# A graph, attention and expert layer on one core: degree factor at the projection's PSUM, and a rewritten end of the edge stage

## The reference

```python
xn = layernorm(x)
# 1. edges
m    = xn[src] @ W[:256] + edge_attr @ W[256:]
deg  = segment_sum(ones, dst)
norm = where(deg > 0, rsqrt(maximum(deg, 1)), 0)
h    = segment_sum(m * norm[dst][:, None], dst) + h_bias
# 2. linear attention, 8 heads of 32, and an MLP
q, k, v = split((xn @ w_qkv + b_qkv) per head);  k, v = ln(k), ln(v)
ret = q @ (k.T @ v / 6250) + xn
mix = gelu(ret @ w1 + b1) @ w2 + b2 + xn
x   = x + h + mix
# 3. two of eight experts, chosen once for all nodes
z      = layernorm(x)
logits = mean(z over nodes) @ Wr + br           # 8 numbers
...                                             # softmax, capacity factor, softmax, top 2, softmax
out    = w_a * expert_a(z) + w_b * expert_b(z)  # 256 -> 512 -> gelu -> 256, each with biases
x      = x + layernorm(out + z) * gamma + beta
```

## Time and profile before

| | |
|---|---|
| runs | 1621.09, 1617.83, 1621.16 us |
| profiled execution | 1610.02 us, span 1608.2 us |
| PE (TensorE) busy | 1053.9 us, 66% |
| DVE (VectorE) busy | 757.3 us, 47% |
| ACT (ScalarE) busy | 537.5 us, 33% |
| POOL (GpSimd) busy | 929.4 us, 58% |
| gathers L550 | 807, 795.7 us, mean 986 ns |
| DMA | 275.65 MB, mean 171 GB/s |

### The profile page before, as it was taken

One profiled execution on the slowest core, in us unless ns is written; L12 is line 12 of the kernel. 1 busy time (PEld: TensorE's weight loads), 2 busy tenths in 40 slices (PEclk: granted clock), 3 DMA queues, 4 the chain that ended last, 5 costly groups with the idle time before them and its releaser, 6 DMA issues.

```text
span 1608.2 us, 19835 instructions
## 1 busy us (share of the span) xinstructions
PE 1053.9 (66%) x5959; PEld 653.6 (41%) x5959; DVE 757.3 (47%) x1755; ACT 537.5 (33%) x1100; POOL 929.4 (58%) x974
## 2 busy tenths in 40 slices
PE   0164766764756665647564775665667649999997
PEld 0021223321322222223331442333333349999997
DVE  5743445553444453522343443443433436677675
ACT  4611111211112111102332333342323357767673
POOL 6166667666676676666666666676665003434342
PEclk9987878787878887778777887887877769999999
DMA  9975555655655565577787777877776031111111
GB/s 222 327 225 181 184 174 178 191 187 177 189 173 180 181 186 185 160 233 211 208 241 228 222 221 221 246 236 219 228 233 184 32 99 27 51 45 44 50 40 40
DMA packets 189375, 275.65 MB, mean 171 GB/s; under 512 B 19840, under 2 KB 160296, under 8 KB 188037
## 3 DMA queue, kind: packets, MB, share of 16 engines
q1 hardware_dynamic: 139424, 152.85, 32.0%
q0 software_dynamic: 39888, 108.97, 22.7%
q10 hardware_dynamic: 9975, 12.80, 2.4%
HBM read 248.95 MB, written 25.60 MB: 171 GB/s over the span
## 4 chain that ended last, share of the span: by engine, by line
another core or an unknown queue 31%; PE 30%; issue 14%; DVE 11%; ACT 8%; DMA 2%; DVEq 2%; SPq 2%; ACTq 0%; POOL 0%; POOLq 0%
PE bank L1093 8%; PE bank L1082 5%; PE ps_t L1082 4%; PE bank L883 3%; PE bank L951 3%; PE bank L906 2%; DVEq L1272 2%; PE bank L982 1%; DVE acc L1274 1%; DVE lnst L1309 1%; DVE nrm L1295 1%; DVE xc L1305 1%; PE bank L994 1%; DMA x<-x 1%
## 5 line engine op out<-in xcount | busy, mean ns | idle before, releaser
L550 POOL DMA_INDIRECT ring<-xn_table,src_sb x807 | 795.7, 986 | 416.4 <-issue 223.4
L883 PE MATMUL bank<-ring,s 128*32 128x512 f32 x1662 | 279.1, 678 | 82.8 <-DVE s L1234 53.3
L951 PE MATMUL bank<-wstage,xt 128*125 128x512 f32 x200 | 133.7, 804 | 145.1 <-ACT xt L616 88.0
L1274 DVE TENSOR_TENSOR acc<-acc,ps_t 128x160 f32 x277 | 89.1, 322 | 133.0 <-issue 87.6
L883 PEld LDWEIGHTS bank<-ring,s 128*32 128x32 f32 x1662 | 41.9, 115 | 204.7 <-issue 141.3
L951 PEld LDWEIGHTS bank<-wstage,xt 128*125 128x125 f32 x200 | 43.6, 242 | 192.9 <-issue 96.8
L1243 DVE TENSOR_TENSOR pair<-s 128x128 f32<-128x128 f32 x70 | 20.2, 288 | 214.0 <-remote 161.5
L1526 DVE TENSOR_TENSOR h_lo<-h,h_hi 128x512 fp32r<-128x512 f32 x100 | 95.7, 968 | 49.2 <-ACT h_hi L616 49.2
L906 PE MATMUL bank<-wg,acc 128*125 128x256 f32 x400 | 101.3, 410 | 25.1 <-DVE acc L1297 19.8
L605 POOL TENSOR_TENSOR rx<-vex,half 125x2 f32<-125x2 f32 x25 | 17.5, 701 | 171.9 <-DVE nmx L1547 171.9
L616 ACT ACTIVATE xt<-bank 128x250 f32<-128x250 f32 (+1 forms) x75 | 33.5, 446 | 236.7 <-remote 198.3
(11 more groups left out here) (210 smaller groups left out, 2253.5 us busy)
## 6 DMA issues: line engine op xcount, KB each, us to landing
ring<-edges SPq DMA_DIRECT2D x207, 512.0 KB
ring<-xn_table,src_sb POOLq DMA_INDIRECT x807
xnr<-xn_table SPq DMA_DIRECT2D x25, 250.0 KB
xch<-x SPq DMA_DIRECT2D x25, 250.0 KB
base_rows<-xch ACTq DMA_DIRECT2D x25, 250.0 KB
xt_cols<-xte ACTq DMA_DIRECT2D x25, 250.0 KB
xtl<-xt_cols SPq DMA_DIRECT2D x25, 250.0 KB, 4.9
out<-res SPq DMA_DIRECT2D x25, 250.0 KB
```

The lines of the kernel that those rows point to most:

```text
L550: pool.indirect_dma_start(out=to, out_offset=None, in_=rows, in_offset=bass.IndirectOffsetOnAxis(ap=index, axis=0),).then_inc(done, 16)
L883: mm = pe.matmul(ps_seg[t % 2][j * W:(j + 1) * W, :], lhsT=s32[:, t % 3, j * TS + i, :], rhs=ring[:, u, j, :], start=i == 0, stop=i == TS ...
L951: mm = pe.matmul(ps_kv[0:TN, :], lhsT=xt[:, n % 2, c, 0:TN], rhs=wstage[:, c, :], start=c == 0, stop=c == KC - 1)
L1274: v.tensor_tensor(acc[:, :, ds(b, W)], acc[:, :, ds(b, W)], planes[:, :, j * W:(j + 1) * W], ALU.add).then_inc(s_acc, 1)
```

## The change

**Degrees.** `nrm` shrinks from 128 x 250 to 125 x 2, one value per node and tile. Two matmuls of one column turn a chunk's counts so that nodes lie on partitions (`turn_degrees`, into spare columns `DEG` of `ps_y`); VectorE takes maximum and reciprocal on 125 x 2 (`degrees`, `inverse_roots`). `scale` and its semaphore are gone: the projection runs on unscaled sums, and ScalarE's `park` applies the factor per partition as it copies from PSUM, in two operations instead of one. The projection moves from the last third of the step after `DONE` to its first third, `park` and `refill` from the step after that to the last third of the same step. `transposes` writes `ps_y` too, so it waits for VectorE's maximum of the chunk before (`s_nrm`). `sums` loads its four addresses ahead of its wait. `refill` stops with chunk 21, as no later sums use those columns.

**End of the edge stage.** `FIN` covers 24 chunks (last entries 67, 70) and the loop ends two steps earlier. TensorE's thirds 207 to 209 and what follows are written out. The last chunk is projected into two other PSUM buffers (`ps_kv`, `ps_acc`), and VectorE applies factor and base rows straight from there (`last_rows`), with the statistics of each tile behind it. Its part of the mean comes from TensorE as `x2` times the row scales (`mean_last`); its turned copy is made during the router (`turn_last`, `keep_last`). The flag is loaded ahead of the loop on every engine (`verdict`). One exponential of a constant is issued ahead of the router's wait.

```diff
-for c in range(NC):
+LAST = NC - 1
+for c in range(LAST):
     FIN.append(max(DONE[c] + 2, FIN[-1] + 1 if c else 0, FIRST + 1 - (-6 * c // 5)))
...
+REFILLS = NC - RC + 1
+EMPTIED = [min(sum(d + 1 <= g for d in DONE), REFILLS) for g in range(NG)]
...
-        nrm = sbe("nrm", [P, CN])
+        nrm = sbe("nrm", [TN, 2])
...
@@ ScalarE @@
             def park(c):
                 act.wait_ge(s_prj, c + 1)
+                act.wait_ge(s_nrm, 2 * c + 2)
                 act.wait_ge(s_xt, 2 * c + 2)
...
-                copy(x2[:, 2 * c:2 * c + 2, :], ps_f[0:TN, :].rearrange("p (t d) -> p t d", t=2)).then_inc(s_park, 1)
+                for j in range(2):
+                    parked = nc.scalar.activation(x2[:, 2 * c + j, :], ps_f[0:TN, j * D:(j + 1) * D], ACT.Copy, scale=nrm[:, j:j + 1])
+                parked.then_inc(s_park, 1)
...
+            def keep_last():
+                u = LAST % 2
+                act.wait_ge(s_ltr, LTR + 1)
+                act.wait_ge(s_te[u], 16 * len(range(u, LAST, 2)))
+                copy(xte[:, u, :, :], ps_xt[:, 0:KC * CN].rearrange("p (c n) -> p c n", c=KC)).then_inc(s_lxe, 1)
+                act.wait_ge(s_lxe, LXE + 1)
+                act.dma_start(xt_d[LAST, :, :].rearrange("p (o n) -> p o n", o=KC), xte[:, u, :, :]).then_inc(s_lte, 16)
...
-                if i == 0 and done_at(t, 1) is not None:
+                if i == 0 and t == NG:
+                    park(LAST - 1)
+                if i == 1 and done_at(t, 1) is not None:
                     degree_roots(done_at(t, 1))
-                if i == 0 and done_at(t, 2) is not None:
-                    park(done_at(t, 2))
-                    refill(done_at(t, 2))
+                if i == 2 and done_at(t, 1) is not None and t < NG - 1:
+                    park(done_at(t, 1))
+                    if done_at(t, 1) < REFILLS:
+                        refill(done_at(t, 1))
...
+            norm_last()
+            nc.scalar.activation(rt[0:1, 15, 0:1], ones[0:1, 0:1], ACT.Exp)
             act.wait_ge(s_sums, 1)
...
             nc.scalar.activation(rt[0:1, 2, :], rt[0:1, 1, :], ACT.Exp, bias=rs[0:1, 1:2]).then_inc(s_ra, 1)
+            keep_last()
             act.wait_ge(s_rd, 16)
@@ TensorE @@
-            def transposes(t):
+            def transposes(t, projected):
                 n = W * len(strips(t))
                 pe.wait_ge(s_cnt, t + 1)
+                wait_past(pe, s_nrm, 2 * projected - 1)
                 wait_past(pe, s_acc, strips_before(t))
                 pe.matmul(ps_y[:, 0:n], lhsT=ones_r[:, :], rhs=counts[:, t % 2, 0:n], start=True, stop=True)
...
-            def project(c):
-                pe.wait_ge(s_scale, c + 1)
-                wait_past(pe, s_park, c)
...
+            def turn_degrees(c):
+                pe.wait_ge(s_acc, min(strips_before(DONE[c]), NS))
+                if c and c % RC == 0:
+                    pe.wait_ge(s_spill, 2 * (c // RC))
                 for j in range(2):
                     a = ring_columns(c) + j * TN
-                    for o in range(2 * KC):
-                        mm = pe.matmul(ps_f[0:TN, j * D:(j + 1) * D], lhsT=acc[:, o, a:a + TN], rhs=wg[:, o, :], start=o == 0, stop=o == 2 * KC - 1)
-                mm.then_inc(s_prj, 1)
+                    mm = pe.matmul(ps_y[0:TN, DEG + j:DEG + j + 1], lhsT=acc[0:1, PLANES - 1, a:a + TN], rhs=ones[0:1, 0:1], start=True, stop=True)
+                mm.then_inc(s_deg, 1)
...
+            def project_both(c):
+                turn_degrees(c)
+                wait_past(pe, s_park, c)
+                project(c, 0, ps_f[0:TN, 0:D])
+                project(c, 1, ps_f[0:TN, D:2 * D]).then_inc(s_prj, 1)
...
+            def mean_last():
+                pe.wait_ge(s_r2, NC)
+                pe.wait_ge(s_park, LAST)
+                for h in range(KC):
+                    ops = [op for t in range(2 * LAST, NT) for op in ((x2[:, t, h * P:(h + 1) * P], r2[:, t:t + 1]), (ones[0:TN, :], nmr2[:, t:t + 1]))]
+                    for n, (a, b) in enumerate(ops):
+                        mm = pe.matmul(ps_f[:, h:h + 1], lhsT=a, rhs=b, start=n == 0, stop=n == len(ops) - 1)
+                mm.then_inc(s_mean, 1)
...
+            for q in range(TS * (NG - 1)):
                 t, i = divmod(q, TS)
-                if q < NQ:
-                    strip_sums(q)
-                if i == 1 and 1 <= t <= NG:
-                    transposes(t - 1)
-                if i == 2 and done_at(t, 1) is not None:
-                    project(done_at(t, 1))
+                strip_sums(q)
+                if i == 1 and t >= 1:
+                    transposes(t - 1, sum(d < t for d in DONE))
+                if i == 0 and done_at(t, 1) is not None:
+                    project_both(done_at(t, 1))
...
+            transposes(NG - 2, LAST - 1)
+            turn_degrees(LAST - 1)
+            pe.wait_ge(s_park, LAST - 1)
+            project(LAST - 1, 0, ps_f[0:TN, 0:D])
+            transposes(NG - 1, LAST)
+            project(LAST - 1, 1, ps_f[0:TN, D:2 * D]).then_inc(s_prj, 1)
+            turn_rows(LAST - 2, NC)
+            turn_degrees(LAST)
+            pe.wait_ge(s_hg, NC)
+            project(LAST, 0, ps_kv[0:TN, 0:D]).then_inc(s_prj, 1)
+            pe.wait_ge(s_bs, NC)
+            project(LAST, 1, ps_acc[0:TN, 0:D]).then_inc(s_prj, 1)
+            turn_rows(LAST - 1, NC)
@@ VectorE @@
             def sums(t):
+                bases = [v.value_load(brow[0:1, t * ST + j:t * ST + j + 1], min_val=0, max_val=RN) for j in strips(t)]
                 v.wait_ge(s_tp, t + 1)
...
             def degrees(c):
-                a = ring_columns(c)
-                v.wait_ge(s_acc, min(strips_before(DONE[c]), NS))
-                v.tensor_scalar(nrm[:, :], acc[:, PLANES - 1, a:a + CN], 1.0, None, ALU.max).then_inc(s_nrm, 1)
-
-            def scale(c):
-                a = ring_columns(c)
+                v.wait_ge(s_deg, c + 1)
+                wait_past(v, s_park, c)
+                v.tensor_scalar(nrm[:, :], ps_y[0:TN, DEG:DEG + 2], 1.0, None, ALU.max).then_inc(s_nrm, 1)
+
+            def inverse_roots(c):
                 v.wait_ge(s_sqd, c + 1)
                 v.reciprocal(nrm[:, :], nrm[:, :]).then_inc(s_nrm, 1)
-                v.wait_ge(s_nrm, 2 * c + 2)
-                v.tensor_tensor(acc[:, 0:2 * KC, a:a + CN], acc[:, 0:2 * KC, a:a + CN],
-                                nrm[:, :].unsqueeze(1).broadcast_to([P, 2 * KC, CN]), ALU.mult).then_inc(s_scale, 1)
...
+            def last_rows():
+                v.wait_ge(s_bs, NC)
+                v.wait_ge(s_nrm, 2 * NC)
+                for j, to in enumerate((ps_kv, ps_acc)):
+                    v.wait_ge(s_prj, NC + j)
+                    v.scalar_tensor_tensor(x2[:, 2 * LAST + j, :], to[0:TN, 0:D], nrm[:, j:j + 1], xch[:, xslot(LAST), j, :],
+                                           ALU.mult, ALU.add).then_inc((s_tile, s_x2)[j], 1)
...
-            general(v, group, start, end, before, again)
-            v.wait_ge(s_xe, NC)
-            v.tensor_reduce(mean_c[:, :], mean_p[:, :, :], AX, ALU.add).then_inc(s_sums, 1)
+            general(v, ok, group, start, end, before, again)
+            v.wait_ge(s_xe, LAST)
+            v.tensor_reduce(mean_c[:, :], mean_p[:, :, :], AX, ALU.add).then_inc(s_part, 1)
+            v.wait_ge(s_part, PART + 1)
+            v.wait_ge(s_mean, MEAN + 1)
+            v.tensor_tensor(mean_c[:, :], mean_c[:, :], ps_f[:, 0:KC], ALU.add).then_inc(s_sums, 1)
```

More of the change, by code:

```diff
@@ L363, in gps_layer, with verdict, general @@
         GE_PASS = 16 * (NG - 1) + 32
-        def general(eng, group, start=None, end=None, before=None, after=None):
+        def verdict(eng):
             eng.wait_ge(s_rel, 1)
-            ok = eng.value_load(ok_i[0:1, 0:1], min_val=0, max_val=1)
+            return eng.value_load(ok_i[0:1, 0:1], min_val=0, max_val=1)
+        def general(eng, ok, group, start=None, end=None, before=None, after=None):
             with eng.If(ok < 1):
@@ L1062, in again @@
             def again(n):
-                turn_rows(n, NC)
-            general(pe, group, start, end, after=again)
+                if n < 2 * NC - 1:
+                    turn_rows(n - 1, NC)
+                else:
+                    pe.wait_ge(s_r2, 2 * NC)
+                    pe.wait_ge(s_xe, 2 * LAST)
+            general(pe, ok, group, start, end, after=again)
+            mean_last()
             pe.wait_ge(s_sums, 1)
@@ L1413, in _ @@
                     variances(kv_at(q, 3))
+                if i == 1 and done_at(t, 1) is not None:
+                    degrees(done_at(t, 1))
+                if i == 2 and done_at(t, 1) is not None:
+                    inverse_roots(done_at(t, 1))
                 if i == 2 and 1 <= t <= NG:
@@ L1418, in _ @@
                         spill(done_at(t, 0))
-                    degrees(done_at(t, 0))
-                if i == 1 and done_at(t, 1) is not None:
-                    scale(done_at(t, 1))
                 if q in (FOLD, FOLD + 2, FOLD + 4, FOLD + 6):
```

108 lines of the change are left out of this document (74 added, 34 removed).

## The result

The changed kernel takes 1609.1 us (median of four runs, 1606.3 to 1609.9) against 1620.4 us before (1617.8 to 1621.2): ratio 0.993, interval 0.9916 to 0.9945, so 11 us less. The forecast was 1605.

The account below looks back on a forecast made before the run. The edge stage was taken as bound by GpSimd's issue first, TensorE's bunched answers second. Edge stage -2 us and end -13.5, rounded to -14, gave -16 from a median of 1621.1: 1605 us, range 1590 to 1624.

Parts of the forecast that it names:

- Step 1: End, first of the two last projections: no longer waits for the multiply, but is split around the last transposes; -1.6 us.
- Steps 2 and 4: End: shorter gap between the last two projections, -7.4 us; mean to first exponential with table loaded ahead, -3.9 us.
- step 3: End, second projection's end to the mean: last chunk's part by matmuls (3.2 us), TensorE's jump partly covered; -0.6 us.
- Step 4's remark on ScalarE: Before the router: ScalarE becomes late next, its table loaded just as the mean arrives; its 3.25 us of idle issue stays.
- -6 from the gathers: Edge stage: without the VectorE multiply, gathers beside it shorten by 0 to 11.6 us; half taken, 6 us.
- +4 from new waits: Edge stage: 10 us more TensorE waiting, of which a third reaches GpSimd, +3 to +4; bounds -7 to +39 us.
- The projection's wait for the sums: Edge stage, TensorE: the earlier projection waits for sums one strip sooner, no longer for the multiply (19.8 us in 5 waits).
- both loosen, both are cover: Edge stage: later refill and copy-out on ScalarE, and address loads ahead of the sums' wait, cost nothing.
- The turned degrees: Edge stage, TensorE: two one-column matmuls per chunk, 0.3 us x 25, costed at nothing.
- rival C: Edge stage: wait before the transposes costs GpSimd a 2.2 us slot wait per chunk; 1627 to 1654 us; chance 0.15.
- The slot waits: Edge stage sign: GpSimd's waits for a free ring slot stay near 155 us; 175 us or more would mean rival C.
- A: Rival, edge stage: GpSimd keeps all 11.6 us and TensorE loses nothing; -26 us, 1595 us; chance 0.22.

Follow-up runs that it names:

- e1: The kernel before, unchanged, run and profiled again on another chip, one without late answers: 1472.4 us.
- e9: The changed kernel, unchanged, a third time, on a chip without slot waits: 1453.0 us against 1476.6 before, ratio 0.9849.
- e11: Changed kernel with projection behind the transposes, address loads between the additions in the loop, one third early for the last three groups: 1448.3 us, ratio 0.982.
- e2: Kernel before with only the edge stage's part of the change; loop, last chunks' order, router and jumps as before: 1457.9 us, ratio 0.9903.
- e10: The same kernel as e2, before plus the edge stage's part alone, in another session: 1457.9 us, ratio 0.9882.
- e4: Changed kernel plus an unused 128x1000 two-input VectorE multiply ahead of the maximum of chunks 1 to 22: 1458.5 us.
- e7: Changed kernel with each group's four address loads one third of a step before its sums: 1588.2 us, ratio 0.9899.
- e5: The changed kernel, unchanged, again, on a chip with slot waits: 1595.1 us against 1604.8 before, ratio 0.994.
- e6: Changed kernel with each address load back between two additions of the sums, as before the change: 1589.6 us, ratio 0.9908.

## Why the prediction came out right, step by step

The end, from the last gather, measured in the timelines (us; the first pair with late answers, the second, e1 and e9, without):

| step | forecast | before, after | change | e1, e9 | change |
|---|---|---|---|---|---|
| 1. first projection ends | -1.6 | 19.9, 20.4 | +0.6 | 11.3, 16.8 | +5.5 |
| 2. gap between the projections | -7.4 | 8.7, 1.6 | -7.1 | 8.7, 1.1 | -7.6 |
| second projection itself | 0 | 5.8, 3.7 | -2.1 | 5.5, 3.7 | -1.8 |
| 3. to the mean | -0.6 | 9.0, 7.1 | -1.9 | 9.0, 6.6 | -2.4 |
| 4. mean to first exponential | -3.9 | 5.3, 1.5 | -3.8 | 5.2, 1.9 | -3.4 |
| to the first expert matmul | 0 | 12.8, 12.8 | -0.1 | 12.9, 12.8 | 0 |
| sum | -13.5 | | -14.4 | | -9.7 |

- Step 1 was wrong in sign. "It is now cut in two around the last transposes, which wait for the sums of group 68, so some 2.3 us go into it": between the halves lie 4.2 us in the trace after (12.6 to 16.8 from the last gather). The step took address loads for gone when they are hoisted; they are on the chain, three of 0.30 us and their issue, 2.5 us. In e11 they are off it, and the gap is 1.2 us against 3.7 in e9. Of e11's 4.7 us at the end that is 2.5; 1.5 more come from the clock of the second half (below), 0.9 from an earlier begin. The ends of single traces hold such terms beside the one that an edit aims at. Against the prediction, the begin was 0.9 us late, the gap 1.9 us too long and the matmuls 0.6 us shorter (5.6 for 6.2).
- Steps 2 and 4 came out within 0.5 us of their sizes. They are the gain.
- The second projection's own length was no term. Before, the granted clock over it was 0.64, so part of it ran at the lower level (0.50, 1.2 GHz); after, it ran at 1.00. In front of it stood 8 us with almost no TensorE work before, and little more than one turn of rows after. But the idling does not decide alone: in e2 and e10, one kernel with the same 6.2 us between the projections, it took 5.3 us (clock 0.69) and 3.7 us (1.00). In all ten traces with the rewritten end it took 3.7. The rows, before and then after, of those matmuls alone:

```profile
1275.92:1281.69 5.77, 5.76 (x16) 4.36 (x16) 0.64 0.00 0
```

```profile
1283.71:1287.43 3.72, 3.72 (x16) 2.92 (x16) 1.00 0.19 69
```

- The clock also took something back in step 1. The first projection's two halves after, eight passes each; the second, behind the gap, ran at the lower level and took 1.6 us more:

```profile
1272.30:1274.30 2.00, 1.99 (x8) 1.42 (x8) 1.00 0.00 0
1278.48:1282.10 3.62, 3.62 (x8) 2.34 (x8) 0.50 0.00 0
```

- In step 3 the sixteen passes of the mean took 3.5 us where 3.2 were taken. The turn of rows ahead of them (0.4 us behind the projection instead of 1.1), TensorE's jump (3.0 instead of 3.7) and the addition (0.1 to its start instead of 0.6) were each shorter.
- Step 4's remark on ScalarE held: the table load ends 0.4 us behind VectorE's answer, and the 3.09 us of idle issue stayed. The early load of the flag moved no jump, as the prediction had it.

The edge stage was forecast at -2: -6 from the gathers and +4 from new waits. The gathers gave 10.7 us of their own time in the first pair and 9.9 in e1 and e9, at the bound of 11.6 rather than its half, and e4 shows that this is the multiply. What was mis-sized is what takes it back. Timed -11.3 and -14.4 at the end leave +3 for the edge stage with late answers, within this pair's spread of some 3 us; without them it is -10. So with late answers the +4 for new waits was too small: +3 and the gathers' 10.7 give about +14, an estimate.

What takes the gathers' gain back there stays open. There are three candidates. The projection's wait for the sums was named and sized low: 48.3 us at L948 for the multiply's 19.8. But in e7 such waits are half those of e5, and the edge stage is as long. The hoisted loads were called "both loosen, both are cover", and cost some 5 us by e6, whose interval overlaps that of e5. The turned degrees were costed at nothing from 0.3 us a chunk, and take 0.73 us: 18.3 us of TensorE in all. The wait in front of the transposes, rival C's place, did not decide: L935 waits for VectorE 9.4 us in six waits.

Most of the prediction's signs held: the router's matmuls start 33.0 us after the last gather instead of 45.8, the gap between the last two projections is 1.6 us, the mean gather 973 ns. The slot waits did not stay.

Of the rivals, A (the edge stage keeps 12 us, 1595) is what happens where TensorE's answers are prompt, with a ratio of 0.985; its price was right and its condition, GpSimd never waiting, was not met in the first session. The sentence that the stage "is bound by GpSimd's issue first and by these answers second" held for both: e1's stage is GpSimd's gathers and issue alone. Rival C's sign in the slot waits came, but its cause and its price of over 1621 us did not.

The forecast was 4 us too fast in all: 5 us short in the edge stage, 1 us the other way at the end. Two errors at the end, +2 us in step 1 and -2 us in the projection's clock, cancelled; the sum is better than its terms. That is luck, and so is the chip: the same prediction, -16 us, would have met -24 on one without late answers.

## What to carry to other kernels

Read whether an engine's waits end in a named releaser or in "remote" before pricing what its faster work is worth: the same 10 to 11 us were kept where answers were prompt and lost where they were late. An address load between operations on VectorE is partly hidden by the operation before it; hoist it only to where the engine idles anyway, a stage earlier and not just ahead of the same wait. Where the last stretch is a serial chain, write it as a list of ends from one common event, in both traces, with the granted clock beside each piece: that shows errors that cancel.

## What the runs showed of the hardware

- One and the same program took 1472.5 us on one chip and 1604.8 us on another, a difference of 9%. Between the traces of before and e1 it is 141 us, 126 of them in the edge stage. On the slower chips TensorE's semaphore updates come microseconds after its matmuls while edges are gathered (over 1 us in 35 of 59 cases in the trace of before), and within 0.05 us from the last gather on.
- A VectorE multiply of 128x1000 from two SBUF inputs, 1.19 us, lengthened the gather beside it in 16 of 22 cases, by 8.1 us in all. A gather that started during the multiply ended 2.0 us after the multiply's start, in 15 of 15 cases.
- Register loads on VectorE: 0.615 us apart in a row, but 0.75 us together with a 128x160 addition of 0.32 us. So four loads and four additions took 4.3 us with the loads ahead and 3.0 us interleaved.
- The same sixteen projection matmuls took 3.7 us at a granted clock of 1.00 and 5.8 us at 0.64.
